# Four heads and four positions in one attention product: B attention of a four-stage transformer kernel on one core

## What is computed

```
x = x + attn_a(layernorm(x))      # softmax over 256 positions, 16 heads of 8, bias per head and distance
x = x + ffn(layernorm(x))         # one shared and the 2 best of 7 routed experts, inner width 352
x = x + attn_b(layernorm(x))      # see below
x = x + ffn(layernorm(x))         # the same weights

def attn_b(query):                          # L, N, E = 32, 256, 128: it attends over the 32 batches
    qkv = einsum('lne,fe->lnf', query, qkv_proj) + qkv_bias
    q, k, v = ...                           # each L x (N * 16 heads) x 8
    attn = softmax(SCALE * einsum('bld,bmd->blm', q, k))        # 32 x 32 for each position and head
    return einsum('lni,ei->lne', mixed, out_proj) + out_bias
```

## Time and profile before

| what | value |
|---|---|
| median of 3 runs | 2832.37 us (2826.76 to 2845.78) |
| profiled execution | 2840.89 us, its span 2839.1 us |
| mean granted TensorE clock | 0.794 |
| instructions | 76148, of them 26854 TensorE products |

### The profile page before, as it was taken

How to read it: one execution, slowest core, us unless ns; L and a number is a source line. 1 busy time by engine, 2 the same in 40 slices (tenths; PEclk the granted TensorE clock), 3 DMA queues, 4 the chain that set the end, 5 groups by cost and what they waited for, 6 DMA issues and landing times.

```text
span 2839.1 us, 76148 instructions
## 1 busy us (share of the span) xinstructions
PE 2338.6 (82%) x26854; PEld 1574.7 (55%) x26854; DVE 1649.9 (58%) x6164; ACT 1342.0 (47%) x2861; POOL 867.0 (31%) x934
## 2 busy tenths in 40 slices
PE   7898989898898996799956768787777878689995
PEld 4565656565565664566534545555555545456663
DVE  3777777777777776455533554444554455445553
ACT  4787878787777774344432221122221222144443
POOL 3111211111111112477760112111112211247776
PEclk7898989898888898899985565565656566589998
DMA  5000000000000000677750000000000000167875
GB/s 198 35 17 19 21 17 19 18 20 17 18 20 18 16 13 29 182 177 181 163 95 10 22 18 22 21 21 20 19 18 22 21 21 18 40 172 177 181 165 94
DMA packets 129156, 168.60 MB, mean 59 GB/s; under 512 B 16240, under 2 KB 101104, under 8 KB 128800
## 3 DMA queue, kind: packets, MB, share of 16 engines
q1 hardware_dynamic: 59168, 118.08, 13.3%
q0 software_dynamic: 51968, 37.26, 8.9%
q10 hardware_dynamic: 17664, 8.39, 1.3%
HBM read 107.55 MB, written 56.12 MB: 58 GB/s over the span
## 4 chain that ended last, share of the span: by engine, by line
PE 56%; issue 15%; POOL 10%; DVE 9%; DMA 4%; ACT 3%; POOLq 1%; ACTq 1%; DVEq 0%; SPq 0%
PE bank_S L1452 6%; POOL out_x L939 5%; POOL x L939 5%; PE bank_E L1461 5%; PE bank_T L1461 5%; PE bank_O L1517 4%; PE bank_O L1475 4%; PE bank_Y L1587 4%; PE bank_E L1535 3%; PE bank_E L1433 3%; PE bank_E L1424 3%; PE bank_E L1536 2%; DMA out_x<-yo,xs 2%; PE bank_E L1537 2%; PE bank_S L1499 2%
## 5 line engine op out<-in xcount | busy, mean ns | idle before, releaser
L980 ACT ACTIVATE z<-z,nm 128x256 f32<-128x256 f32 x1024 | 441.0, 500 | 114.8 <-DVE nm L1203 113.9
L1203 DVE CUSTOM_DVE_ANT_0 z<-bank_S,big 128x256 f32<-128x256 f32 x1024 | 380.7, 421 | 185.5 <-PE bank_S L1452 132.7
L875 POOL DMA_INDIRECT sent<-rows,slots x256 | 249.8, 976 | 248.8 <-DVE slots L1279 173.9
L1356 DVE SCALAR_TENSOR_TENSOR both<-both,bank_E 128x512 f32<-128x512 f32 (+1 forms) x228 | 155.6, 682 | 236.0 <-ACT both L1036 235.9
L939 POOL DMA_INDIRECT x<-yo,xs x152 | 237.1, 1560 | 121.9 <-DMA x<-yo,xs 43.3
L939 POOL DMA_INDIRECT out_x<-yo,xs x152 | 236.1, 1553 | 122.4 <-issue 48.7
L1452 PE MATMUL bank_S<-kx,qx 32*128 32x256 f32 x1024 | 212.5, 370 | 73.9 <-issue 32.9
L860 POOL COPY seen<-seen 128x8 f32<-128x8 f32 x32 | 6.1, 192 | 750.0 <-DVE picked L1170 714.2
L1452 PEld LDWEIGHTS bank_S<-kx,qx 32*128 32x128 f32 x1024 | 129.7, 213 | 160.1 <-issue 91.7
L1535 PE MATMUL bank_E<-xbh,w_gu 128*128 128x512 f32 (+1 forms) x342 | 178.4, 522 | 38.7 <-DMA w_gu<-w_split 25.5
L1517 PE MATMUL bank_O<-vx,probT 32*32 32x9 f32 x8192 | 120.9, 190 | 96.7 <-DVE probT L1237 85.1
(11 more groups left out here) (188 smaller groups left out, 5068.0 us busy)
## 6 DMA issues: line engine op xcount, KB each, us to landing
w_gu<-w_split SPq DMA_DIRECT2D x76, 704.0 KB, 5.4
xs<-sent SPq DMA_DIRECT2D x76, 264.0 KB, 2.8
w_dn<-w_split SPq DMA_DIRECT2D x76, 192.0 KB, 5.3
w_split<-w_gu SPq DMA_DIRECT2D x7, 704.0 KB, 3.1
both<-in_w_raw SPq DMA_DIRECT2D x8, 544.0 KB, 4.7
xin<-in_x SPq DMA_DIRECT2D x16, 256.0 KB, 2.9
sent<-rows,slots POOLq DMA_INDIRECT x256
x<-xo ACTq DMA_DIRECT2D x16, 256.0 KB, 2.3
```

The lines of the kernel that those rows point to most:

```text
L875: pool.indirect_dma_start(out=sent, out_offset=bass.IndirectOffsetOnAxis(ap=slots[:, n:n + 1], axis=0), in_=rows[:, k, t, :], in_offset=No ...
L980: last = act.activation(zt, zt, ACT.Exp, bias=nm[:, n % NM_RING, t:t + 1], scale=-1.0)
L1203: last = dve.tensor_tensor_reduce(z[:, n % Z_RING, t * SEQ:(t + 1) * SEQ], bank[s][:, t * SEQ:(t + 1) * SEQ], bias_a[:, h, P - P * t:P - P ...
L1356: dve.scalar_tensor_tensor(out=a, in0=a, scalar=1.0, in1=in_blocks(q)[0:m, :], op0=ALU.add, op1=ALU.mult).then_inc(ba_ready, 1)
```

## The change

Only B passes compute otherwise; the orders of the A rounds are the same as before.

- A product now takes four heads and four positions at once. `quads` and `by_quad` number positions as 16 pass + 4b + a: b is a slot, a a place in it. For every b and group g of heads, q_wide has the 8 numbers of four heads in the quarter of the partitions that belongs to place a, with zeros elsewhere, and 128 columns (a, batch); k_wide holds for each of four heads h a copy of k in which only the rows of h are kept, 128 columns (h, batch). bscores is then 16 products of 128 x 128 with a contraction over 128.
- qk: a product of four rows adds the bias in PSUM, and 16 products on a quarter of the array's columns put each place a in its quarter. ScalarE writes q in four copies and k in four (`widen`). The spread steps and the cut in high and low part are gone in B.
- v: a one-row product adds the bias, and ScalarE makes four copies into v_wide, which is 0 outside the place's own quarter.
- bmix: 16 products of 128 x 128, and 16 with a 4-column 0/1 operand for the sums (bank E2, which B had not used in its passes). ScalarE takes the 16 wanted pieces out of the four banks; VectorE divides once.
- bturn goes by E2, bout is 16 products on 32 rows each into four banks, and VectorE adds them in four instructions.
- The residual rows are loaded once more in the new numbering (xkeep, four DMAs on SP's queue), and keep reads those. The output is stored in that numbering.
- The wide buffers of B are cleared once by GpSimd at the start of the A blocks. Buffers q_wide and k_wide are single, where qx and kx were double.

```diff
-CHAIN = {"Y": 4, "PY": 2, "Q0": 1 + GROUPS, "Q1": 1 + GROUPS}
-        "B": {"S0": 2, "S1": 1, "T": 2, "O": 1 + TOK, **CHAIN}}
+        "B": {"S0": 3, "S1": 3, "T": 3, "O": 3, "E2": 2, "Q0": 1, "Q1": 1, **CHAIN}}
...
-    "bscores": {"pe": 0.5, "dve": 1.4, "act": 0.5}, "bprobs": {"dve": 0.6}, "bmix": {"pe": 0.35, "dve": 0.6},
+    "bscores": {"pe": 1.1, "dve": 1.4, "act": 0.6}, "bprobs": {"dve": 0.6},
+    "bmix": {"pe": 1.6, "act": 1.2, "dve": 1.0},
...
+                for b in range(TOK):
+                    sp.dma_start(xkeep[32 * b:32 * b + 32, :, :], quads(x2[0:MOST, :], p.by(1), b)
+                                 ).then_inc(xkeep_landed, 16)
...
+                if kind == "A":
+                    pool.memset(big[:, 0:WIDE], 0.0)
+                    pool.memset(v_room[:, :], 0.0).then_inc(cleared, 1)
...
+            def widen(p, n):
...
+                src = bank[f"Q{n}"][:, :].rearrange("p (g b l) -> p g b l", g=GROUPS, b=TOK)
+                for k in range(4):
+                    if n == 0:
+                        r = slice(32 * k, 32 * k + 32)
+                        last = act.activation(q_wide[r, :, :, k, :], src[r], ACT.Copy, scale=SCALE)
+                    else:
+                        last = act.activation(k_wide[:, :, :, k, :], src, ACT.Copy, scale=cst[:, C_HH + k:C_HH + k + 1])
+                last.then_inc(emptied[f"Q{n}"], 1)
...
+                    for a in range(4):
+                        r = slice(32 * a, 32 * a + 32)
+                        src = bank["PY"][r, :].rearrange("p (x d) -> p x d", d=DH)
+                        dst = v_wide[r, :, :, :, a, :].rearrange("p b g h d -> p (b g h) d")
+                        last = act.activation(dst, src, ACT.Copy)
...
+                    for h in range(4):
+                        r = slice(32 * h, 32 * h + 32)
+                        src = bank[s][r, :].rearrange("p (g h x) -> p g h x", g=GROUPS, h=4)[:, :, h, :]
+                        dst = ctx_mixed[r, n * P:(n + 1) * P].rearrange("p (a g d) -> p g a d", a=4, g=GROUPS)
+                        last = act.activation(dst, src.rearrange("p g (a d) -> p g a d", a=4), ACT.Copy)
...
+                    if p.kind == "B":
+                        alone(pe)
+                        pe.matmul(bank[f"Q{n}"][:, :], brow[:, n, :], spread(ident[0:GROUPS, 0:GROUPS], 2, P), start=True,
+                                  stop=False)
+                        for g in range(GROUPS):
+                            for a in range(4):
+                                last = pe.matmul(bank[f"Q{n}"][32 * a:32 * a + 32, g * P:(g + 1) * P],
+                                                 proj[:, half, n, 32 * g:32 * g + 32], by_quad(xnT[:, :])[:, a],
+                                                 start=False, stop=(g == GROUPS - 1),
+                                                 tile_position=(0, 32 * a))
...
+                        pe.matmul(bank["PY"][:, :], ones[0:1, :], spread(bc[0:1, P:2 * P], 1, TOK), start=True, stop=False)
...
+                        last = pe.matmul(bank[s][:, g * P:(g + 1) * P], q_wide[:, g, n].rearrange("p a l -> p (a l)"),
+                                         k_wide[:, g, n].rearrange("p h l -> p (h l)"), start=True, stop=True)
...
+                    for g in range(GROUPS):
+                        a = probT[:, n, g * P:(g + 1) * P]
+                        last = pe.matmul(bank[s][:, g * P:(g + 1) * P], a,
+                                         v_wide[:, n, g].rearrange("p h a d -> p (h a d)"), start=True, stop=True)
+                    last.then_inc(filled[s], 1)
+                    for g in range(GROUPS):
+                        a = probT[:, n, g * P:(g + 1) * P]
+                        sums = bank["E2"][:, n * HEADS:(n + 1) * HEADS].rearrange("p (a g) -> p g a", g=GROUPS)[:, g, :]
+                        last = pe.matmul(sums, a, cst[:, C_QUAD:C_QUAD + 4], start=True, stop=True)
...
+                    for h in range(4):
+                        for a, s in enumerate(B_BANKS):
+                            r = slice(32 * a, 32 * a + 32)
+                            last = pe.matmul(bank[s][:, 0:P], ctx_turned[r, h * P:(h + 1) * P], proj_o[r, h, :],
+                                             start=(h == 0), stop=(h == 3), tile_position=(32 * a, 0))
```

More of the change, by code:

```diff
@@ L268, in needs_before @@
     if step in ("turn2", "twin", "keep") and eng in ("pe", "pool"):
-        return [("dve", "norm2", last)] + ([("dve", "v", 0)] if step == "turn2" else [])
+        return [("dve", "norm2", last)] + ([("dve" if kind == "A" else "act", "v", 0)] if step == "turn2" else [])
     if step == "begin" and eng == "pool":
@@ L361, in work @@
     def work(t):
-        return rule["work"].get((t[0], t[1]), WORK[t[1]][t[0]])
+        return WORK_B[t[0:2]] if kind == "B" and t[0:2] in WORK_B else WORK[t[1]][t[0]]
     everything = {e: [list(steps) for steps in left[e]] for e in FLOW}
@@ L1495, in attention @@
+                    next_use(p, s, 0)
                     for g in range(GROUPS):
-                        c = (t * GROUPS + g) * 32
-                        for j in range(4):
-                            lo = t * P + 32 * j
-                            last = pe.matmul(bank[s][32 * j:32 * j + 32, c:c + 32], qx[rows, p.two, g, lo:lo + 32].bitcast(F32),
-                                             kx[rows, p.two, g, lo:lo + 32].bitcast(F32), start=True, stop=True,
-                                             tile_position=(32 * r, 32 * j))
@@ L1510, in attention @@
+                    pe.wait_ge(turned, p.count({"A": 0, "B": TOK}, n + 1))
+                    if n == 0:
                         pe.wait_ge(emptied["PY"], use(p, "PY", 1))
-                        next_use(p, "O", 1 + t)
-                        alone(pe)
-                    c = (t * GROUPS + g) * 32
-                    for h in range(4 * g, 4 * g + 4):
-                        for j in range(4):
-                            r = slice(32 * j, 32 * j + 32)
-                            last = pe.matmul(bank["O"][r, h * VW:(h + 1) * VW], probT[r, h % 4, c:c + 32],
-                                             vx[r, p.two, t, h * VW:(h + 1) * VW], start=True, stop=True,
-                                             tile_position=(32 * j, 32 * j))
@@ L1524, in attention @@
-                    turn_rows(p, ctxb, "T", 1)
+                    pe.wait_ge(mixed, p.count({"A": 0, "B": 1}, 1))
+                    turn_rows(p, ctx_mixed.rearrange("p (b c) -> p b c", b=TOK), "E2", 1)
                 elif step == "bout":
-                    pe.wait_ge(emptied["T"], use(p, "T", 1))
-                    next_use(p, "S0", last_use(p, "S0"))
-                    for t in range(TOK):
-                        last = pe.matmul(bank["S0"][:, t * P:(t + 1) * P], ctxT[:, t * P:(t + 1) * P], proj_vo[:, 2, :],
-                                         start=True, stop=True)
```

238 lines of the change are left out of this document (150 added, 88 removed).

## The result

The changed kernel takes 2754.8 us (median of 4 runs, 2749.2 to 2758.2) against 2832.9 us (4 runs, 2826.8 to 2845.8): a ratio of 0.972 with a 95% interval of 0.968 to 0.975. It is 78 us faster, where 129 us were forecast; 2755 us lies inside the range and inside the forecast's own range of 2640 to 2770 us.

The account below looks back on a forecast made before the run. TensorE was taken as the bound, at a low clock in B passes with small products and issue gaps. 15.5 passes going from 58.3 to 50.0 us save 129 us, giving 2704 us; range 2590 to 2815.

Parts of the forecast that it names:

- The pass before: 58.3 us: One B pass of the unchanged kernel, taken as 700 us of window divided by 12 passes.
- The pass after: 50.0 us: One changed B pass: 40.5 us at 2.4 GHz, low-clock charges of 2, 5 and 2, and 0.5 for loop issue.
- rival 1: B passes: the clock never drops for long; 41.5 us a pass, 2572 us in all; chance 0.14.
- The prediction's line 41 + 19.7 f: Length in us of a changed B pass when a fraction f of it runs at the low clock.
- I charge for the first 2 us: Pause around the turned rows: half of the projections priced at the low clock, 2 us a pass.
- rival 3: Changed B passes: the clock stays low; 60.2 us plus the loop's 0.5 a pass, 2869 us; chance 0.13.
- four fifths low: Mix and sums after the second pause: four fifths at the low clock, 5 us on top of 8.0.
- The sums: 0.46 us a product low, 0.25 high: 16 four-column products in the mix stage: 0.46 us each at the low clock, 7.4 us together; 0.25 each high.
- I take the first: Output product cut into 16 on 32 rows: four run side by side, costing as before, 1.0 or 1.9 us.
- Rival 2: Packed products don't run side by side: pass 59 us, 2843 us in full; chance 0.06; output product alone 2750.
- The scores stage, 14.4 us with VectorE setting its end: First scores to first mix product: VectorE has 13.2 us of work at the high clock before the transposed bank.
- 15.5 passes x 8.3: Total gain: 14 looped passes plus filling and draining, each going from 58.3 to 50.0 us, 129 us.

Follow-up runs that it names:

- e10: Changed kernel plus unread products filling TensorE's pauses: 4 ahead of the turned rows, 8 behind, ten before the mix; 2569.0 us, ratio 0.903 to the kernel before.
- e3: Changed kernel with the 16 sums' products at 128 columns instead of 4, so the divisor differs; 2624.8 us, ratio 0.923 to the kernel before.
- e4: Changed kernel plus ten unread 512-column products in TensorE's pause before the first mix product; 2619.7 us, ratio 0.920 to the kernel before.
- e1: Changed kernel with bias products contracting over 128 rows instead of 4 or 1, same sums; 2693.3 us, ratio 0.946 to the kernel before.
- e8: Kernel before the change plus 22 unread 512-column products in its 5.6 us pause ahead of the mix; 3123.3 us, ratio 1.0053, on the late-issue chip.
- e2: Changed kernel with the bias of q, k and v left out in B passes; 2664.1 us, ratio 0.936 to the kernel before.
- e12: Changed kernel with bias added on VectorE and unread products around the turned rows, behind v and before the mix; 2601.0 us, ratio 0.914 to the kernel before.
- e11: Changed kernel with bias added on VectorE and ten unread products before the mix; 2596.9 us, ratio 0.912 to the kernel before.
- e5: The same kernel as e10, run earlier on the chip with late issues; 2807.3 us, ratio 0.904 to the kernel before.

## Why the prediction was right or wrong

The direction, its reason (the issue gaps and small products go, full products at a higher mean clock come) and the range held; the size was 129 us forecast for 78 measured, 82.7 in the spans. That the time lies inside the forecast's own range is partly luck. A pass was taken too short both before (by 2.3 us) and after (by 4.7); with the true pass before, the same working gives 15.5 x 10.6 = 164 us, twice what was measured. And the prediction's own signs of being right failed: a mean clock of 0.66 for 0.70 to 0.85, a pass of 54.7 us for 46 to 54, q and k at 3.9 us each for 1.9 to 3.7.

1. *The pass before: 58.3 us, from "96 products ... at eight a pass, so it is 12 passes".* Too short. Twelve groups of eight fit into a stretch of 11.6 periods when it begins ahead of one and ends behind another. The starts of the turned rows give 60.6 us, 2.3 us more, in favour of the change.
2. *The pass after: 50.0 us.* It is 54.7. This is the step that failed, and almost all of it is the clock charge, not the prices. With the clock high e10 has 42.1 us a pass, where 40.5 at 2.4 GHz throughout and 41.5 for rival 1 stood; e3 and e4, where the clock is high in most of the mix or all of it, have 8.4 and 7.2 us for mix and sums (8.0 predicted), 9.5 and 9.6 for the end (8.8). The prediction's line 41 + 19.7 f gives 54.4 us at the measured clock (0.66, so f = 0.68): taken together the prices of the two levels were right, the share of the time at the low one was not.
3. *"I charge for the first 2 us (half of the projections at the low price)."* This term was the largest miss: the stage took 14.3 us, 5.0 over its high price, and even 0.8 over the low one. It rested on "full products lift it" and on rows 8, where two full projections brought the clock back. But the change had put products of four rows and of one row ahead of and between them, and quarter-width ones behind. e1 shows it: the same count, all 128 rows, and the stage falls to 12.0 us, the next one by 1.3. The prediction named four-row bias products in rival 3, set against it that the projections lifted the clock at once in B, which only full ones had done, and gave them no charge of their own.
4. *Mix "four fifths low", 5 us; the end 2 us.* Measured 13.7 us for 13.0, and 12.0 for 10.8: the low stretch reached on into the downs, until 1931 us. The charge was right in kind. But "it is the 32x32 products that held it down" is half the cause at most: in e8 the mix loses a high clock, though where its small products come with gaps between them, while in the changed kernel full products with thin ones between them don't regain it either.
5. *The sums: 0.46 us a product low, 0.25 high.* Measured 0.39 (1913.83 to 1915.40 for four) and 0.20 (e4), so 6.3 and 3.2 us a pass. The row of L1548 was a good neighbour. The estimate from the 60 cycles a matmul of the Trainium skill (TensorEngine Tiling, Instruction Overhead), 1.6 us for all 32 halves, is a quarter of what the runs show at that clock.
6. *Packing: "I take the first".* Right: 16 row-packed products in 1.1 us, and 16 column-packed ones in 1.08 at 2.4 GHz (e10), 1.94 at 1.2. Rival 2 falls, and no cost of the changes of tiling mode is to be seen beyond the 0.21 us of issue ahead of the row-packed ones.
7. *The scores stage, 14.4 us with VectorE setting its end.* 14.7, which is luck in part: that is at a mean clock of 0.85, and at 0.98 (e1) the stage takes 13.4. The price was 1 us too high, and the low clock at the stage's start, for which nothing was charged, made up for it. *Widening on ScalarE hidden:* true for the changed kernel, where TensorE waits for no copy; e2 and e12 show that it is next in line. *Loads of residual rows: nothing.* xin comes 5.2 us a pass late for VectorE and the slack of 4.6 us behind it stays. *Loop issue, 0.5 us:* the passes alternate by 0.2 us at most, so less than that.
8. *"15.5 passes x 8.3".* 82.7 us of span over 5.9 us a pass are 14.0 passes. The 13 periods from the third turned rows of B to the last gave 71 us (781.7 to 710.4), the way from there to the last rank 12 (75.0 to 62.7); the third turned rows themselves come 1.5 us later (1609.4 for 1607.9), so the passes being filled gained nothing that shows, those being drained did. Of the 46 us missing in the span, 37 are the 2.4 us a pass (4.7 too low after, 2.3 too low before), 9 the passes counted too many.

What drops the clock before the mix is narrowed down but not settled. In the changed kernel it falls in the pause itself, some 0.9 us ahead of the first mix product (1911.97), with TensorE all but idle:

```profile
1910.00:1912.00 2.00, 0.03 (x1) 0.04 (x1) 1.84 (x6) 0.93 (x2) 0.00 (x0) 0.77 0.00 0
```

With the pause filled it never falls there (e4). With the pause as it was and full-width sums (e3) it falls in seven passes of twelve and is back within the stage. So the pause drops it, and the thin sums keep it from coming back. Why the same pause leaves it high in the other five passes of e3 is open.

## What to carry to other kernels

Price each stage at both clocks, and charge the low one from a pause until *full* products, 128 rows deep, have brought the clock back; four-row or one-row products behind a pause keep the low clock, and in e10 a high clock fell among them in eight passes of twelve, so give them full depth (e1: 2.6% less time for the same work, by the two ratios). Where a pause of 2 to 3 us can't be removed, unread products in it can pay (e4: 5%, e10: 6.7%), as long as they end before the real operands are ready: in e12 they overran and held the mix up by 2.6 us a pass. Where another engine's chain is the bound, they bring nothing: the first stage took 11.7 us in e11 at a clock of 0.71 to 0.75 and in e12 at 1.00. Take a period from the first and last start of one instruction, not from a count in a window.

## What was not expected of the hardware

- A product with 4 columns cost nearly what one with 128 did, both with a full 128x128 fp32 stationary operand: 0.95 us for four against 1.06 (e4, e3).
- At the same instruction count, the granted clock depended on how many rows the products contract over (e1): bias products over 4 and 1 rows ran at 0.50 for 8 us, over 128 rows the second one was already partly fast (1.69 us for 2.05).
- More work can be less time: ten added products of 512 columns, 2.5 us, shorten a pass by 9.5 us, because the 6.5 us of mix and sums saved and 2.4 of the end are all clock (e4 against the changed kernel).
- Products over 4 and 1 rows also went with the loss of a high clock, without any pause: in e10 in eight passes of twelve, in e12, which has none of them, in no pass of twelve.
- On one chip of those used the kernel before took 3105.8 us, 9% longer than on the others, with long waits of the issue kind. The ratio of the same kernel (e5, e10) was nevertheless 0.904 and 0.903.
